# The expert stage of a two-layer transformer kernel: hidden transposes one block later, evictions of the down product a block later

## What is computed

```python
logits = x @ gate_weight.T
topk_w, topk_idx = top_k(softmax(logits), 8)          # 64 experts, 8 for each row
topk_w = topk_w / sum(topk_w)
g = ragged_dot(sorted_rows, w_gate, group_sizes)      # 512 -> 192
u = ragged_dot(sorted_rows, w_up, group_sizes)        # 512 -> 192
out = ragged_dot(silu(g) * u, w_down, group_sizes)    # 192 -> 512
y = sum(outs * topk_w)                                # the 8 results of a row
```

## Time and profile before

| | us |
|---|---|
| median of 3 runs (lowest to highest) | 1588.92 (1582.53 to 1594.41) |
| the profiled execution | 1586.65 |
| its span | 1584.8 |
| TensorE busy in the span | 1416.3 (89%) |
| VectorE busy | 1032.9 (65%) |
| ScalarE busy | 904.0 (57%) |

### The profile page before, as it was taken

How to read it: one execution, slowest core, us unless ns; L and a number is a source line. 1 busy time by engine, 2 the same in 40 slices (tenths; PEclk the granted TensorE clock), 3 DMA queues, 4 the chain that set the end, 5 groups by cost and what they waited for, 6 DMA issues and landing times. The chain is left out here.

```text
span 1584.8 us, 37524 instructions
## 1 busy us (share of the span) xinstructions
PE 1416.3 (89%) x8673; PEld 1192.8 (75%) x8674; DVE 1032.9 (65%) x2067; ACT 904.0 (57%) x2048; POOL 614.6 (39%) x704
## 2 busy tenths in 40 slices
PE   7999899989734999999999999999953599999999
PEld 5887566657523898898988898888842488888888
DVE  5555588866686676777777666666635476667632
ACT  5555699864294666666666666665621244444442
POOL 1222488751241322322232332222226566666322
PEclk9999799999855999999999999999986799999999
DMA  6221791001261587878787877777547444444200
GB/s 219 82 86 53 280 358 35 2 5 60 84 275 60 187 281 262 293 243 298 255 284 249 272 251 258 272 246 244 199 156 247 141 140 139 138 123 128 74 13 28
DMA packets 93284, 278.19 MB, mean 176 GB/s; under 512 B 12757, under 2 KB 12886, under 8 KB 92502
## 3 DMA queue, kind: packets, MB, share of 16 engines
q1 hardware_dynamic: 69526, 199.67, 35.8%
q0 software_dynamic: 23680, 77.61, 16.2%
HBM read 209.07 MB, written 76.81 MB: 180 GB/s over the span
## 5 line engine op out<-in xcount | busy, mean ns | idle before, releaser
L1205 POOL DMA_INDIRECT xg<-h_rows,idx x168 | 186.0, 1107 | 461.7 <-PE m_x L1243 452.3
L1258 PE MATMUL m_g<-wgu_high,bxTh 128*128 x660 | 235.8, 357 | 2.7 <-DVE bxTl L1329 2.7
L1258 PE MATMUL m_g<-wgu_low,bxTh 128*128 x660 | 223.4, 338 | 0.0
L1258 PE MATMUL m_g<-wgu_high,bxTl 128*128 x660 | 223.1, 338 | 0.0
L1655 PE MATMUL f_g<-x4T_high,ffn_gu 128*128 128x256 f32 x704 | 175.6, 292 | 13.9 <-DVE f_hid L1827 12.2
L1329 DVE TENSOR_TENSOR bxTl<-m_x,bxTh 128x512 fp32r<-128x512 f32 x166 | 114.7, 691 | 83.5 <-ACT bxTh L1396 71.9
L1655 PE MATMUL f_g<-x4T_low,ffn_gu 128*128 128x256 f32 x704 | 169.0, 281 | 0.0
L1063 DVE TENSOR_TENSOR wgu_low<-raw_gu,wgu_high x61 | 107.3, 1759 | 82.4 <-ACT wgu_high L1053 76.5
L1414 ACT ACTIVATE y<-m_y 128x512 f32<-128x512 f32 x164 | 98.3, 599 | 109.2 <-PE m_y L1278 77.2
L1546 POOL DMA_INDIRECT G<-y_rows,slot x128 | 132.2, 1033 | 51.1 <-issue 46.0
L1278 PE MATMUL m_y<-wd_high,hidTm 128*128 x328 | 143.9, 439 | 5.4 <-DVE hidTm L1343 3.6
(11 more groups left out here) (264 smaller groups left out, 3269.1 us busy)
## 6 DMA issues: line engine op xcount, KB each, us to landing
raw_gu<-in_exp_gu SPq DMA_DIRECT2D x64, 768.0 KB, 6.7
y_rows<-y SPq DMA_DIRECT2D x164, 256.0 KB
raw_d<-in_exp_d SPq DMA_DIRECT2D x64, 512.0 KB, 7.5
y_rows<-zero SPq DMA_DIRECT2D x64, 256.0 KB, 3.4
ffn_gu<-ffn_gu_words SPq DMA_DIRECT2D x1, 5632.0 KB, 22.2
raw_c<-in_ctxT SPq DMA_DIRECT2D x16, 256.0 KB, 2.6
X<-in_x SPq DMA_DIRECT2D x4, 1024.0 KB, 5.3
h_rows<-h SPq DMA_DIRECT2D x16, 256.0 KB, 2.0
```

The source lines that it names most:

```text
L1205: eng.indirect_dma_start(xg[:, u, :].bitcast(F32), None, h_dram, bass.IndirectOffsetOnAxis(ap=idx[half][:, u:u + 1], axis=0)).then_inc(s_g ...
L1258: m = eng.matmul(pg[u % 2][:, 0:2 * I], xT[l][:, u % 2, c, :], W.gu[r][:, buf * DC + c, :], start=c == 0 and n == 0, stop=c == DC - 1 and ...
```

## The change

TensorE's iteration becomes: row transposes of b+2, hidden transposes of b-1 (one block later than before, right behind the row transposes), gate and up of b+1 with the table entry of b+2 loaded between its second and third chunk, down product of b-1. Two waits go (`hid` of b-1 ahead of gate and up, `lows` of b-2 ahead of the hidden transposes), the values of the waits are worked out once per group, and `lows` count one step per block, not two. ScalarE's iteration becomes: `highs` of b-1, rows' higher half of b+2, `out` of b-2, table entry, weights, silu of b+1. VectorE's becomes: `lows` of b-1, rows' lower half of b+2, table entry, weights, `hid` of b+1; the word bits of a group then stand between `hid` of its fifth block and `lows` of its last. VectorE's first group is taken out of its loop. After the loops the last hidden transposes, `lows`, `highs`, and two evictions follow.

```diff
@@ block.tensor @@
-            def turn(b, u, n):
-                eng.wait_ge(s_g[u], n * 16)
-                dveX.wait(eng, b - 2, "xTl")
+            def turn(u, landed):
+                eng.wait_ge(s_g[u], landed)
...
-                for sem, value in needed:
-                    eng.wait_ge(sem, value)
-                dveH.wait(eng, b - 2, "h")
+                eng.wait_ge(W.s_low_gu, split)
+                eng.wait_ge(dveX.sem, turned)
                 for c in range(DC):
                     for n, (l, r) in enumerate(THREE):
...
+                    if c == 1:
+                        result = beside()
...
-            def turn_hidden(b, u):
+            def turn_hidden(u, hidden):
                 par = u % 2
-                dveH.wait(eng, b, "h")
-                dveT.wait(eng, b - 2, "hTl")
+                eng.wait_ge(dveH.sem, hidden)
...
                 W.ready_d(eng, e)
-                dveT.wait(eng, b, "hTl")
-                actY.wait(eng, b - 2, "y")
+                eng.wait_ge(dveT.sem, split)
+                eng.wait_ge(actY.sem, out)
...
-            def one(i, u, before, following):
-                b = i * GB + u
-                needed = needs(b + 1, following[0])
-                turn(b + 2, (u + 2) % GB, i + 1 + (u + 2) // GB)
-                gate_up(b + 1, (u + 1) % GB, *following, needed)
-                after = entry(eng, b + 2)
-                turn_hidden(b, u)
+            def one(i, u, before, this, following, values, landed):
+                split = eng.snap(following[0] + 1)
+                turn((u + 2) % GB, landed[(u + 2) // GB])
                 if before is not None:
-                    down(b - 1, (u - 1) % GB, *before)
+                    turn_hidden((u - 1) % GB, values[u + 2])
+                after = gate_up((u + 1) % GB, *following, split, values[u + 4], lambda: entry(eng, i * GB + u + 2))
+                if before is not None:
+                    down((u - 1) % GB, *before, values[u + 2], values[u])
                 return after
...
             def group(i, before, this, following):
+                at = eng.snap(i * GB) if before is not None else 0
+                values = [eng.snap(at + value(d)) if before is not None else value(d) for d in range(-3, GB + 1)]
+                landed = [eng.snap(i * 16 + n) if before is not None else n for n in (16, 32)]
@@ block.vector @@
-            def one(b, u, before):
+            def one(b, u, before, first):
+                if not (first and u == 0):
+                    lows(b - 1, (u - 1) % GB)
                 turned(b + 2, u + 2)
                 e = begun(eng, b - 1)
                 split_next(eng, before, b - 2, W.low_d)
                 split_next(eng, e, b - 1, W.low_gu)
                 hidden(b + 1, u + 1)
-                lows(b, u)
                 return e
@@ block.scalar @@
             def one(i, u, before, first):
                 b = i * GB + u
+                if not (first and u == 0):
+                    highs(b - 1, (u - 1) % GB)
                 turned(b + 2, u + 2)
+                if not (first and u < 2):
+                    out(b - 2, (u - 2) % GB, None if first else i * 32 + u // 2 * 16)
                 e = begun(eng, b - 1)
                 split_next(eng, before, b - 2, W.high_d)
                 split_next(eng, e, b - 1, W.high_gu)
                 silu(b + 1, u + 1)
-                highs(b, u)
-                if not (first and u == 0):
-                    out(b - 1, (u - 1) % GB, None if first and u < 3 else i * 32 + (u + 1) // 2 * 16)
                 return e
```

More of the change, by code:

```diff
@@ L1133, in experts @@
         peH, peY = Steps(nc, ctx, "m_peH", ["hT"]), Steps(nc, ctx, "m_peY", ["y"])
-        dveX, dveH, dveT = Steps(nc, ctx, "m_dveX", ["xTl"]), Steps(nc, ctx, "m_dveH", ["h"]), Steps(nc, ctx, "m_dveT", ["hTc", "hTl"])
+        dveX, dveH, dveT = Steps(nc, ctx, "m_dveX", ["xTl"]), Steps(nc, ctx, "m_dveH", ["h"]), Steps(nc, ctx, "m_dveT", ["hTl"])
         actX, actS = Steps(nc, ctx, "m_actX", ["xTh"]), Steps(nc, ctx, "m_actS", ["silu"])
@@ L1244, in turn, with gate_up @@
                 peX.done(m, "xT")
-            def needs(b, e):
-                return [(sem, eng.snap(value)) for sem, value in ((W.s_low_gu, e + 1), (dveX.sem, dveX.value(b, "xTl")))]
-            def gate_up(b, u, e, buf, needed):
-                for sem, value in needed:
-                    eng.wait_ge(sem, value)
-                dveH.wait(eng, b - 2, "h")
+            def gate_up(u, e, buf, split, turned, beside):
+                eng.wait_ge(W.s_low_gu, split)
+                eng.wait_ge(dveX.sem, turned)
                 for c in range(DC):
@@ L1259, in gate_up, with down @@
                                        start=c == 0 and n == 0, stop=c == DC - 1 and n == 2)
+                    if c == 1:
+                        result = beside()
                 peG.done(m, "g")
-            def turn_hidden(b, u):
+                return result
+            def turn_hidden(u, hidden):
                 par = u % 2
-                dveH.wait(eng, b, "h")
-                dveT.wait(eng, b - 2, "hTl")
+                eng.wait_ge(dveH.sem, hidden)
                 eng.transpose(ph[par][:, 0:P], hid[:, par, 0:P], ident[:, :])
                 peH.done(eng.transpose(ph[par][0:IB, P:2 * P], hid[:, par, P:I], ident[:, :]), "hT")
-            def down(b, u, e, buf):
+            def down(u, e, buf, split, out):
                 par = u % 2
                 W.ready_d(eng, e)
-                dveT.wait(eng, b, "hTl")
-                actY.wait(eng, b - 2, "y")
+                eng.wait_ge(dveT.sem, split)
+                eng.wait_ge(actY.sem, out)
                 (high, low), at = W.d, buf * 2
@@ L1303, in group @@
             def group(i, before, this, following):
+                at = eng.snap(i * GB) if before is not None else 0
+                values = [eng.snap(at + value(d)) if before is not None else value(d) for d in range(-3, GB + 1)]
+                landed = [eng.snap(i * 16 + n) if before is not None else n for n in (16, 32)]
                 for u in range(GB):
-                    after = one(i, u, before, following)
+                    after = one(i, u, before, this, following, values, landed)
                     before, this, following = this, following, after
@@ L1314, in _ @@
             used = used_groups(eng, endb)
-            group(0, None, (e, buf), entry(eng, 1))
+            group(0, None, (e, buf), after)
             each_group(eng, 1, used, lambda i: group(i, *taken()))
-            down(eng.snap(used * GB - 1, min_val=T * K // P - 1, max_val=NBLK - 1), GB - 1, *taken()[0])
+            last = eng.snap(used * GB - 1, min_val=T * K // P - 1, max_val=NBLK - 1)
+            turn_hidden(GB - 1, eng.snap(value(last)))
+            down(GB - 1, *taken()[0], eng.snap(value(last)), eng.snap(value(last - 2)))
         @block.vector
@@ L1341, in lows @@
                 peY.wait(eng, b - 2, "y")
-                dveT.done(eng.tensor_tensor(hidTl[:, par, :], ph[par][:, 0:P], hidTm[:, par, 0, :].bitcast(F32), ALU.subtract), "hTc")
+                eng.tensor_tensor(hidTl[:, par, :], ph[par][:, 0:P], hidTm[:, par, 0, :].bitcast(F32), ALU.subtract)
                 dveT.done(eng.tensor_tensor(hidTm[IB:P, par, 1, :], ph[par][0:IB, P:2 * P], hidTm[0:IB, par, 1, :].bitcast(F32), ALU.subtract), "hTl")
@@ L1362, in one, with bits_of, blocks, group @@
                 hidden(b + 1, u + 1)
-                lows(b, u)
                 return e
-            def group(i):
+            def bits_of(i, chunk):
+                dveB.wait(eng, i - 1, "bits")
+                dveB.done(eng.tensor_tensor(low_bits[:, :], low_bits[:, :], all_bits[:, bass.ts(chunk, D)], ALU.bitwise_or), "bits")
+            def blocks(i, first):
                 before = begun(eng, i * GB - 2)
                 for u in range(GB):
-                    before = one(i * GB + u, u, before)
+                    before = one(i * GB + u, u, before, first)
+            def group(i):
+                blocks(i, False)
                 with eng.If(i < 2 * FC):
-                    dveB.wait(eng, i - 1, "bits")
-                    dveB.done(eng.tensor_tensor(low_bits[:, :], low_bits[:, :], all_bits[:, bass.ts(eng.snap(i % (2 * FC), min_val=0, max_val=2 * FC - 1), D)], ALU.bitwise_or), "bits")
+                    bits_of(i, eng.snap(i % (2 * FC), min_val=0, max_val=2 * FC - 1))
             used = used_groups(eng, endb)
-            begin = 0
+            blocks(0, True)
+            bits_of(0, 0)
+            begin = WORDS_AT[0]
             for r, chunks in enumerate(rounds):
-                with eng.Fori(begin, WORDS_AT[r]) as i:
-                    group(i)
+                if begin < WORDS_AT[r]:
+                    with eng.Fori(begin, WORDS_AT[r]) as i:
+                        group(i)
                 eng.wait_ge(s_words[r], 16 * len(chunks))
@@ L1386, in _ @@
             each_group(eng, begin, used, group)
```

(6 more changed lines are left out.)

7 lines of the change are left out of this document (4 added, 3 removed).

## The result

| | before | after |
|---|---|---|
| median (lowest to highest), us | 1586.13 (1582.53 to 1594.41) | 1611.12 (1606.13 to 1621.37) |
| the profiled execution, us | 1586.65 | 1608.91 |
| its span, us | 1584.8 | 1607.1 |

Four runs of each; the ratio is 1.0158, 95% interval 1.013 to 1.0186. The change makes the kernel slower by some 25 us of median, 22.3 us between the two profiled executions. The forecast was 1612 us.

What follows compares the result with a forecast made beforehand. TensorE was taken to bound the expert stage, 22.5 us lost to late VectorE results. New losses 21.4 + 7.4 + 10 + 8 + 1 = 47.8 us, so +25.3 on 1586.65: 1612 us (range 1570 to 1634, own range 1600 to 1630).

Steps and rivals of the forecast that it cites:

- A: Expert stage: `wgu_high` not delayed, `lows` keep their time, the 22.5 us lost go; about 1567 us, chance 0.18.
- B: Expert stage roughly even: `wgu_high` delayed 0.16 to 0.3 us, losses 20 against 22.5, about 1584 us; chance 0.26.
- C: TensorE register work bounds: each of 41 groups exposes 1.2 us, 49 instead of 10, about 1651 us; chance 0.06.
- Neighbours of the transposes: TensorE's new order beside the small transposes: neither cost nor gain, taken as 0 us.
- The bound of 18: TensorE's small transposes: new neighbours could cost or win 0.11 us per block, 164 x 0.11 = 18 us at most.
- Split blocks: Blocks with a gate and up split: `wgu_high` 0.51 us later, down product 0.35 us late, 61 times, 21.4 us.
- Word bits: VectorE's low-bit merges, now ahead of `lows`, uncovered behind a split: 33 x 0.61 x 0.37 = 7.4 us.
- Register work at group ends: TensorE's sequencer after waiting for `lows`: 0.65 us exposed in 15 groups, 10 us (0 to 49).
- its upper end: Group-end register work at most 41 x 1.2 = 49 us, including the table load uncovered after a late block.
- rival B's second figure: Group register work hidden by a deep TensorE lead, other terms as forecast: 37.8 - 22.5, 1602 us; chance 0.10.
- Store waits: Waits of `y` for its store stay, since store and reuse move alike, now ahead of the weight split: 8 us.
- The ends: At the stage's end the last block's `lows` and a second eviction stand alone: 1 us.

## Why the prediction was right

The direction, the place and the size came out: 1611 us where 1612 was forecast, and it is not the rivals A, B or C. The forecast was worked out from one profiled execution, 1586.65 + 25.3; between the two profiled executions it is 22.3 us. In the forecast's own terms, over 3.86 us a block, 47.8 us were to be lost and 673.1 - 629.2 = 43.9 were: 52.1 over the shorter block, less 8.2 won. The terms were off in both directions, and the agreement within a few us is partly luck:

- *Neighbours of the transposes, costed at 0*: they won 8.2 us. The bound of 18 held. The run with the trimmed sequence in the old order shows that it is the order; why is not shown.
- *Split blocks, 61 x 0.35 = 21.4 us*: about 29 (27.8 + 11 x 0.56, less 4.7 that belongs to the register work below). The step that was wrong is the delay of `wgu_high`. I took the sequencer's 1.45 us plus 0.15 from `highs`, 1.60; it is 1.42. In the block shown above, `wgu_high` starts 676.48 - (672.99 + 0.17) = 3.32 us after gate and up (672.99 is the start of their last product), where it was 672.39 - 669.35 = 3.04: 0.28 us later, not 0.51. (Both are blocks behind one that was not late.) `lows` end 0.01 to 0.03 us after gate and up in the last two blocks of a group, and the down product is then 0.22 to 0.27 us late. What I had not seen is that the load follows `lows` by more than 0.15 us in the other two. The sequencer's own rows of lines 1272, 1273 and 1278, for the block shown above and for the block at 672 us:

```profile
L1272 PEldq EVENT_SEMAPHORE  x1: 51/51/51, 682.0 to 682.0; - x1
...
L1273 PEldq ALU_OP  x1: 32/32/32, 682.2 to 682.2; - x1
...
L1278 PEldq FUSED_REGOPS  x2: 55/55/55, 682.2 to 682.5; - x2
...
L1273 PEldq EVENT_SEMAPHORE  x1: 531/531/531, 671.8 to 671.8; - x1
...
L1278 PEldq FUSED_REGOPS  x2: 55/55/55, 672.4 to 672.6; - x2
```

  In the first, `lows` end at 682.00, and a wait and an addition still stand between that and the load's registers; in the second the instruction that waits (531 ns) is the last one, and the registers follow it. So the first two blocks of a group, of the first kind, are 0.36 and 0.45 us late (medians, without word bits). The two errors nearly cancel.
- *Word bits, 7.4 us*: 17.6 - 11 x 0.56 = 11.4, and 9.2 in the run that moves them. A split and word bits met for 16 instructions (6 + 5 x 2), where I took 33 x 0.37 = 12; 16 x 0.61 is 9.8 us, so the duration was right and the count too low. Of the 11.4 us about 1.2 are the lower clock in one of these blocks.
- *Register work at group ends, 10 us*: about 7.6. A split block at a group's end takes 4.48 us, one of the same lateness in the middle 4.12: 0.36 us more, 13 times, 4.7 us; the blocks at a group's end that are not split add 2.9. The row for it is PEld's wait for "issue" at the row transposes: 21.7 us in 18, of which 16.2 are one wait at the start of the stage, so 5.5 us in 17, where the kernel before has 18.6 - 16.2 = 2.4 us in 5. That is the smaller part. By the starts on PE, gate and up of a group's first block begin 2.0 us later in all, and another 4.7 us go inside gate and up, in 22 groups, where the table entry stands; the row is PEld's wait for "issue" there, 6.9 us in 24. One of them, the table load at TensorE's sequencer and the weight load behind it:

```profile
L1144 PEldq TENSOR_LOAD <-blk_tab x1: 311/311/311, 663.0 to 663.0; - x1
...
663.82 0.19 PEld L1254 LDWEIGHTS m_g<-wgu_high,bxTh 128*128 128x128 f32 x1 [0.24 <-issue]
```

  So in a group's first block the table load inside gate and up is not hidden, which the forecast had kept for its upper end, and the moves and branches at the group's end cost less than was put down for them. The sequencer has a short lead, and rival B's second figure (1602 us, this term at 0) did not come. The Trainium skill ("TensorE: Matmul & The Clock Gate", section "Architectural detail: the array is 16× 32×32, not 1× 128×128") gives TensorE's queue 64 entries. By that, the prediction says, this work would always be hidden; the trace disagrees by these 7.6 us, and the measurement decides. How deep the queue is, no run here measures: in a late block the sequencer stands in the wait for `lows` and TensorE runs dry, so that nothing was queued.
- *Store waits, 8 us*: they fell to 3.6 us in the whole stage. "Store and reuse move alike" was wrong. They come back (10.1, 14.6 us) in the two runs with the entry ahead and the eviction behind the silu, and stay (20.2 and 30.5 us) in the old order. But 16.0 us in 9 blocks stand in the last run with later splits too, whose eviction was not moved, and only 6.6 in the run that moves the eviction alone, so the eviction's place by itself does not decide it. What does was not tested, and stays open.
- *The ends, 1 us*: about 3.

Rival A's ground, that ScalarE no longer sits in a 77.2 us wait, is true of the row and of no use: the wait for the hidden transposes, 211.6 us, took its place. What A needed was a `wgu_high` that starts no later than before; the run with the entry ahead and the eviction behind has that, and still only reaches the kernel before, 1587 us and not 1567, since the late blocks there still lose 27.6 us over 3.81: 8.7 of them in the 11 blocks with word bits, 13.2 in the other 50 with a split, of which 15 are still late. Why those 15 are late is not shown.

The best version is neither kernel: the old order with ScalarE's eviction a block later, 1581 us.

## What to carry to other kernels

Moving an operation a block later moves its consumers' deadline too: look for what is produced *behind* it on the next engine (here `lows` behind `hid` and a split) and compare that with the new deadline, not only the wait that goes. When an instruction starts late on an engine, ask for both limits, the work ahead of it on the engine and the register work ahead of it in its sequencer; taking away the smaller one, or one of two equal ones, wins little, and here 5 and 13 us alone made 24 together. Where a change has several parts, run each by itself: here a part that won 7 us alone stood inside a change that lost 25.

## What the runs showed of the hardware

- Six transposes in a row, four of rows and two of hidden values, and only then the big products: a block costs 0.05 us less than with two separate groups of four and two (3.81 against 3.86 and 3.87), with the same products and the same granted clock.
- ScalarE's evictions follow each other by 0.28 us (128x256) and 0.48 us (128x512), though their rows show 0.38 and 0.60 us each.
- A load of the table entry and the addresses behind it hold a ScalarE instruction back: it starts 1.41 us after the eviction that had waited, when that one (128x256) and one of 128x512 stand ahead of it; with the load moved ahead of the wait it is 0.76 us, the two evictions' own 0.28 + 0.48.
- TensorE's granted clock fell from 1.00 to 0.50 in one block of the stage, behind 1.8 us in which the engine stood idle; a product then took 629 ns where its like take 390 to 402 at 1.00. In another block late by 1.9 us it stayed at 1.00.
